# An attention and mixture-of-experts layer on one core: TensorE's scores products and values products stand between single items of the maximum pass, the latter in two parts

## The chip, the cores and the metric

The kernel runs on one core of one Trainium2 chip. The metric is the device time of one execution in microseconds (us); smaller is better.

## The reference

One layer on x of shape (4, 1024, 128), float32, with 16 heads of width 8, and then a mixture of 8 experts of which each token takes 2. Cut to what matters:

```python
Q, K, V = (proj(W_Q), proj(W_K), proj(W_V))          # (4, 16, 1024, 8)
Q = _apply_rope(Q, cos, sin)
K = _apply_rope(K, cos, sin)
scores = jnp.einsum('bhsd,bhtd->bhst', Q, K) / jnp.sqrt(jnp.float32(D_K))
scores = jnp.where(causal[None, None], scores, -jnp.inf)
attn = jax.nn.softmax(scores, axis=-1)
out = jnp.einsum('bhst,bhtd->bhsd', attn, V)
...
x = _layernorm(x + _L0_attn_ref(x, W_Q, W_K, W_V, W_O), axis=-1)
x = _layernorm(x + _L0_ffn_ref(x, Wg, bg, W1, b1, W2, b2), axis=-1)   # 8 experts, hidden 512, top 2
```

## The kernel before, in words

The attention works in 16 units, each of one batch and four heads. A unit is gone over twice. The **maximum pass** (events A, lines L703 to L708 on TensorE, L1157 on VectorE) computes the scores with the queries on the partitions and takes each query's maximum over the keys. It has 40 items per unit. An item is one head (or two, where the widths are small) of one block of 128 queries against up to 512 keys; its products fill one bank of a ring of three PSUM banks, and VectorE reduces that bank in one instruction. Where a block touches the diagonal, two small products (L703, L705) lay the mask under it first. The **second pass** computes the scores again, transposed, with the keys on the partitions and the maximum already subtracted (event QK, L734, two for each step, one for each pair of heads), takes the exponential on ScalarE (L867), cuts the diagonal block on GpSimd (L1408) and multiplies by the values (event PV, L754).

The second pass of a unit is 12 steps: for the first 512 queries four blocks of keys with 512, 384, 256 and 128 queries left of the diagonal, for the second 512 queries four with 512 and then four with 512, 384, 256 and 128. While the second pass of unit u runs, the maximum pass of unit u+1 is spread over its steps by a_quota, 1 to 5 items to a step (40 in all, as [4, 7, 10, 11, 15, 20, 24, 28, 33, 36, 38, 40] adds them up).

All engines walk the same written list of events (schedule()), each taking its own. So the order on every engine is fixed by that list, and an instruction that waits holds up all that stands behind it on its engine. In one step the list has: QK of the next step for the first pair of heads, half of the step's items, QK for the second pair, the other half, and then PV of the step before. PV is four products, one for each head, that stand side by side in the array's four groups of 32 columns (tile_position (0, 32 h)), float32, so that the trace shows eight instructions; QK and the items use the two halves of 64 rows, bfloat16: parity 0 of the heads lies on rows 0 to 63 and parity 1 on rows 64 to 127, so that two of different parity can run side by side.

What the waits in TensorE's list are: an item waits until VectorE has read the bank that it goes to (ring_read); QK i waits for the exponential of QK i-2 (exp_done); PV waits for both exponentials of its step, or for the two cuts on GpSimd where the step touches the diagonal (masked), and the first PV of each half of the queries waits in addition until ScalarE has copied the previous sum out of the one accumulator bank (ot_ready, event EV, L875). Beside these there are two small transposes a unit of the maxima (MT, L716, which wait for four small operations on GpSimd, L1379 to L1385, event SPLIT) and two of the results (OT, L763). From unit 4 on, the rest of the layer for the batch before (projection, norm, gating, scatter of the tokens by indirect DMA, L1394) is spread over the steps as well, and VectorE and TensorE have more to do; the steps from the last of unit 3 to the last but one of unit 11 are a loop body that runs twice. Unit 15 has no items beside it. After the attention come 72 tiles of the experts, which the change leaves alone.

Of the kernel before, what the change touches and what calls it, by code (L numbers as in the profile page):

```python
# [33 lines left out]
NG = H // GH  # L34
CH = 512
NCH = B * S // CH
# [54 lines left out]
B_STEPS = pass_b_steps()  # L91
NA, NB = len(A_ITEMS), len(B_STEPS)
NU = B * NG
C_LAST = [max(k for k, st in enumerate(B_STEPS) if st[0] == c) for c in range(2)]
# [5 lines left out]
def diagonal(k):  # L100

    c, j, s0, n = B_STEPS[k]
    return s0 == P * j


DIAG = [sum(diagonal(i) for i in range(k + 1)) for k in range(NB)]
# [5 lines left out]
    return [NA * sum(work[:i + 1]) // sum(work) for i in range(len(work))]  # L112


def schedule():

    quota = a_quota()
    ev = []
    ev.append(("VX", 0))
    first = next(k for k in range(NB) if quota[k] >= A_HALF)
    ev += [("A", 0, i) for i in range(A_HALF)] + [("SPLIT", 0, 0)]
    middle = (A_HALF + NA) // 2
    ev += [("A", 0, i) for i in range(A_HALF, middle)] + [("MT", 0, 0), ("MROWS", 0, 0)]
    ev += [("A", 0, i) for i in range(middle, NA)] + [("SPLIT", 0, 1)]  # L130
    ev += [("QK", 0), ("QK", 1)]

    def after(bt):

        order = [
            [("T1", bt, 0)], [("T1", bt, 1)], [("WO", bt, 0)], [("WO", bt, 1)],
            [("LNM", bt, 0)], [("LNM", bt, 1)], [("LNV", bt, 0)], [("LNR", bt, 0)], [("LNR", bt, 1)],
            [("LNA", bt, 0)], [("LNA", bt, 1)], [("T2", bt, 0)], [("T2", bt, 1), ("XC", bt), ("LG", bt, 0)], [("LG", bt, 1)],
            [("RA", bt, 0)], [("RX", bt), ("RS", bt, 0)], [("RB", bt, 0)], [("RB", bt, 1)],
            [("RC", bt, 0)], [("RC", bt, 1)], [("RK", bt, 0), ("RK", bt, 1)], [("RD", bt, 0)], [("RD", bt, 1)],  # L140
            [("RE", bt, 0)], [("RE", bt, 1)], [("RF", bt, 0)], [("RF", bt, 1)],
        ] + [[("SC", bt, i)] for i in range(2 * BT)] + ([[("SW", bt)]] if bt < B - 1 else [])
        plan = {3 + i: events for i, events in enumerate(order)}
        return plan

    for u in range(NU):
        for k in range(NB):
            step = u * NB + k
            items = []
            if u + 1 < NU:  # L150
                items = [("A", u + 1, n) for n in range(quota[k - 1] if k else 0, quota[k])]
            half = len(items) // 2
            if k == NB - 1 and u % NG == 3:
                ev.append(("MARK", u))
            if step + 1 < NU * NB:
                ev.append(("QK", 2 * step + 2))
            ev += items[:half]
            if step + 1 < NU * NB:
                ev.append(("QK", 2 * step + 3))
            ev += items[half:]  # L160
            if u + 1 < NU and k in (first, NB - 1):
                ev.append(("SPLIT", u + 1, int(k == NB - 1)))
            if step:
                ev.append(("PV", step - 1))
                if (step - 1) % NB in C_LAST:
                    ev.append(("EV", 2 * ((step - 1) // NB) + C_LAST.index((step - 1) % NB)))
            for back in (0, 1):

                if step >= 3 and (step - 3) % NB == C_LAST[back]:
                    ev.append(("OT", 2 * ((step - 3) // NB) + back))  # L170
            if k == 2 and u + 2 < NU:
                ev.append(("LOAD", u + 2))
            if k == 5 and u + 1 < NU:
                ev.append(("VX", u + 1))
            if k == first + 1 and u + 1 < NU:
                ev += [("MT", u + 1, 0), ("MROWS", u + 1, 0)]
            if k == 0:
                ev += [("MT", u, 1), ("MROWS", u, 1)]
            if u >= NG:
                ev += after(u // NG - 1).get(u % NG * NB + k, [])  # L180
            if u == NU - 1 and k == 4:
                ev.append(("TA",))
    last = NU * NB - 1
    ev += [("PV", last), ("EV", 2 * NU - 1), ("OT", 2 * NU - 1)]
    ev.append(("END",))
    for i, (_, events) in enumerate(sorted(after(B - 1).items())):
        ev += [("TILE", i)] + events

    r, out = 0, []
    for e in ev:  # L190
        if e[0] in ("A", "MT", "OT", "T1", "WO", "T2", "LG", "RK"):
            out.append((e, r))
            r += 1
        else:
            out.append((e, None))
    return out, r
# [75 lines left out]
def build(nc, xT, x, w, wg, bg, w1, w2,  # L272
          cs, ident, halves, maskA, before, tile128, tokens, tiles, first_row, out):
    ctx = ExitStack()
    with ctx:
# [140 lines left out]
        v_read = sem("v_read")  # L416
# [232 lines left out]
        def _(pe):  # L649
# [34 lines left out]
            def visit(e, r, at):  # L684
# [52 lines left out]
                elif kind == "PV":  # L737
                    u, k = divmod(e[1], NB)
                    c, j, s0, n = B_STEPS[k]
                    if e[1] == 0:  # L740
                        pe.wait_ge(v_read, NCH)
                    if k == 0:
                        pe.wait_ge(vx_ready, at(u + 1, NG))
                    if j == 0 and 2 * u + c > 0:

                        pe.wait_ge(ot_ready, at(2 * u + c, 2 * NG))
                    if diagonal(k):
                        pe.wait_ge(masked, at(2 * (u * DIAG[-1] + DIAG[k]), 2 * NG * DIAG[-1]))
                    else:
                        pe.wait_ge(exp_done, at(2 * e[1] + 2, 2 * NB * NG))  # L750
                    for slot_ in (0, 1):
                        for par in (0, 1):
                            h = 2 * slot_ + par
                            last = mm(pv[32 * h:32 * h + 32, s0 - c * CH:s0 - c * CH + n],  # L754
                                      vx[:, u % NG, j, h, :], probs[(2 * e[1] + slot_) % 6][:, par, 0:n],
                                      start=(j == 0), stop=(k == C_LAST[c]),
                                      tile_position=(0, 32 * h), skip_group_check=True)
                    last.then_inc(pv_done, 1)
                elif kind == "OT":
                    n = e[1]  # L760
                    pe.wait_ge(ot_ready, at(n + 1, 2 * NG))
                    for t in range(4):
                        last = nc.tensor.transpose(ring[:, bank, t * P:(t + 1) * P],  # L763
                                                   ot[:, n % 2, t * P:(t + 1) * P], id_sb[:, :])
                    last.then_inc(ring_full, 1)
                elif kind == "LG":
                    bt, c = e[1:]
                    pe.wait_ge(ring_read, at(RING_OF[("T2", bt, c)] + 1, RING_BATCH))
                    for t in range(4):
                        last = mm(ring[:, bank, t * E:(t + 1) * E], aT[:, c, t * P:(t + 1) * P], wg_sb[:, :],  # L770
                                  start=(t == 0), stop=True, skip_group_check=True)
                    last.then_inc(ring_full, 1)
                elif kind == "RK":

                    pe.wait_ge(top_mask, at(e[1] + 1, 1))
                    mm(ring[:, bank, 0:BT * E], before_sb[:, e[2], :], rt[:, 4, :, :], start=True, stop=True
                       ).then_inc(ring_full, 1)
                elif kind in ("T1", "WO", "T2"):
                    bt, c = e[1:]
                    if kind == "T1":  # L780

                        pe.wait_ge(ring_read, at(RING_OF[("OT", 2 * NG * bt + 2 * NG - 1)] + 1, RING_BATCH))
                    elif kind == "WO":
                        pe.wait_ge(ring_read, at(RING_OF[("T1", bt, c)] + 1, RING_BATCH))
                    else:
                        pe.wait_ge(x1_done, at(2 * bt + c + 1, 2))
                    for t in range(4):
                        cols = slice(t * P, (t + 1) * P)
                        if kind == "T1":
                            last = nc.tensor.transpose(ring[:, bank, cols], attn[:, 4 * c + t, :], id_sb[:, :])  # L790
                        elif kind == "WO":
                            last = mm(ring[:, bank, cols], aT[:, c, cols], w_sb[:, 5, :], start=(t == 0), stop=True,
                                      skip_group_check=True)
                        else:
                            last = nc.tensor.transpose(ring[:, bank, cols], xr[:, 4 * c + t, 0, 0:D], id_sb[:, :])
                    last.then_inc(ring_full, 1)
# [717 lines left out]
```

## Time and profile before

| | |
|---|---|
| median of 3 runs | 820.85 us (820.37 to 832.62) |
| the profiled execution | 823.58 us, span in the trace 821.8 us |
| TensorE (PE) busy | 683.3 us, 83% |
| VectorE (DVE) busy | 584.6 us, 71% |
| ScalarE (ACT) busy | 443.5 us, 54% |
| GpSimd (POOL) busy | 320.7 us, 39% |
| granted clock of TensorE | 0.90 on average |
| the attention's 16 units | about 74 to 592 us of the span |

"Busy" counts the time in which at least one instruction of the engine was under way. Products on TensorE are pipelined, and each row of it lasts longer than the distance to the next one's start; distances between starts tell what one costs when others follow.

### The profile page before, as it was taken

What the parts mean: (1) busy time and instruction counts of PE and PEld (TensorE: products, weight loads), DVE (VectorE), ACT (ScalarE), POOL (GpSimd) and SP (SyncE); (2) the same over time, 40 slices, a digit from 0 to 9 for tenths busy, and PEclk for the clock granted to TensorE, in tenths of its full rate; (3) what the DMA queues carried; (4) which work ended last, traced back from release to release, by engine and by line L of the source; (5) the groups of instructions that cost most, each with busy time, mean ns of one, the idle gap of its engine ahead of it and who ended that gap; (6) DMA issues with size and microseconds to landing.
All of it is one profiled execution on the core that took longest, in us unless ns stands there. A gap on an engine that the chain in (4) does not pass through costs nothing.

```text
span 821.8 us, 18980 instructions
## 1 busy us (share of the span) xinstructions
PE 683.3 (83%) x5560; PEld 362.6 (44%) x5561; DVE 584.6 (71%) x1467; ACT 443.5 (54%) x840; POOL 320.7 (39%) x577
## 2 busy tenths in 40 slices
PE   7987999999898868989889998988789857899830
PEld 3432333334343222434323333332278857798830
DVE  7886888888979867798988888896436712222266
ACT  2532676666455554556557655556647524466524
POOL 5961223322213265221328512226614555344551
PEclk9975999999879988998989998899989968899985
DMA  8893255011010120101012011000186745687923
GB/s 274 267 343 125 72 132 162 8 46 48 1 48 6 49 74 22 48 1 48 7 47 80 25 38 46 1 3 22 34 211 200 209 122 147 174 225 210 300 85 114
DMA packets 67352, 83.70 MB, mean 102 GB/s; under 512 B 9266, under 2 KB 46776, under 8 KB 67264
## 3 DMA queue, kind: packets, MB, share of 16 engines
q1 hardware_dynamic: 62912, 74.04, 30.5%
q0 software_dynamic: 4352, 8.53, 3.0%
q8 instruction: 49, 0.80, 0.4%
q14 instruction: 39, 0.32, 0.1%
HBM read 55.77 MB, written 26.90 MB: 101 GB/s over the span
## 4 chain that ended last, share of the span: by engine, by line
PE 50%; DVE 22%; issue 9%; ACT 5%; DMA 4%; SPq 4%; another core or an unknown queue 3%; POOL 2%; DVEq 0%; ACTq 0%; POOLq 0%
PE banks L754 14%; DVE mx L1157 14%; PE banks L708 9%; PE banks L823 6%; PE banks L734 5%; PE banks L812 5%; PE banks L703 2%; PE banks L763 2%; ACT region L867 2%; PE banks L655 2%; DMA region<-pairs 1%; ACT x_sb L910 1%; PE banks L832 1%; SPq L597 1%
## 5 line engine op out<-in xcount | busy, mean ns | idle before, releaser
L1157 DVE TENSOR_REDUCE mx<-banks 128x1 f32<-128x512 f32 (+3 forms) x640 | 366.0, 630 | 46.9 <-PE banks L708 41.5
L867 ACT ACTIVATE region<-banks 128x1024 f32<-128x1024 f32 (+3 forms) x256 | 201.3, 840 | 169.4 <-PE banks L734 159.7
L708 PE MATMUL banks<-region 64*128 64x512 bf16 (+3 forms) x768 | 196.0, 352 | 17.2 <-DVE mx L1157 15.1
L734 PE MATMUL banks<-region 64*128 64x512 bf16 (+3 forms) x768 | 141.6, 347 | 20.7 <-ACT region L867 11.4
L754 PE MATMUL banks<-region 128*32 128x512 f32 (+3 forms) x1024 | 123.1, 555 | 0.9 <-POOL region L1408 0.8
L867 ACT ACTIVATE cs_sb<-banks 128x1024 f32<-128x1024 f32 (+2 forms) x128 | 91.2, 759 | 42.4 <-PE banks L734 41.8
L1418 POOL DMA_INDIRECT results<-region,dest x72 | 71.7, 996 | 105.1 <-DVE region L1285 71.9
L703 PE MATMUL banks<-mask_sb,half_sb 64*128 64x128 bf16 (+1 forms) x384 | 84.7, 252 | 22.6 <-DVE mx L1157 17.3
L1279 DVE TENSOR_TENSOR region<-banks,w1e 128x128 f32<-128x128 f32 x72 | 21.0, 291 | 110.8 <-PE banks L812 66.3
L823 PE MATMUL banks<-region,w1e 128*128 128x128 f32 x576 | 83.2, 291 | 19.3 <-ACT region L893 13.9
L1408 POOL TENSOR_SCALAR_AFFINE_SELECT region<-region 128x256 f32<-128x256 f32 x160 | 64.2, 410 | 87.7 <-ACT region L867 85.1
L734 PEld LDWEIGHTS banks<-region 64*128 64x128 bf16 x768 | 42.4, 95 | 122.9 <-issue 47.3
L1408 POOL TENSOR_SCALAR_AFFINE_SELECT cs_sb<-cs_sb 128x256 f32<-128x256 f32 x96 | 38.6, 412 | 143.4 <-ACT cs_sb L867 142.6
L708 PEld LDWEIGHTS banks<-region 64*128 64x128 bf16 x768 | 65.2, 100 | 56.0 <-DVE mx L1157 42.9
L812 PE MATMUL banks<-w_sb,region 128*128 x576 | 83.3, 290 | 3.9 <-issue 1.8
L823 PEld LDWEIGHTS banks<-region,w1e 128*128 128x128 f32 x576 | 75.9, 205 | 21.4 <-ACT region L893 15.6
L901 ACT ACTIVATE region<-banks,w1e 128x128 f32<-128x128 f32 x288 | 82.9, 379 | 0.5 <-PE banks L823 0.5
L812 PEld LDWEIGHTS banks<-w_sb,region 128*128 128x128 f32 x576 | 74.3, 200 | 8.1 <-issue 6.7
L1394 POOL DMA_INDIRECT pairs<-xT_sb,slot x64 | 63.0, 985 | 36.9 <-issue 21.8
L705 PE MATMUL banks<-mask_sb,half_sb 64*128 64x64 bf16 (+1 forms) x384 | 71.3, 209 | 0.0
L893 ACT COPY region<-banks 128x128 f32<-128x128 f32 x72 | 19.2, 267 | 93.1 <-PE banks L832 67.5
L703 PEld LDWEIGHTS banks<-mask_sb,half_sb 64*128 64x128 bf16 x384 | 35.2, 97 | 61.9 <-DVE mx L1157 46.4
(177 smaller groups left out, 687.8 us busy)
## 6 DMA issues: line engine op xcount, KB each, us to landing
w1e<-in_w SPq DMA_DIRECT2D x72, 322.0 KB
region<-stack_q SPq DMA_DIRECT2D x64, 112.0 KB
region<-stack_k SPq DMA_DIRECT2D x32, 224.0 KB
region<-pairs SPq DMA_DIRECT2D x72, 66.0 KB
region<-results SPq DMA_DIRECT2D x8, 512.0 KB, 4.9
stack_q<-x_sb SPq DMA_DIRECT2D x8, 384.0 KB, 3.6
stack_k<-x_sb SPq DMA_DIRECT2D x8, 384.0 KB, 4.5
stack_q<-x_sb SPq DMA_DIRECT2D x8, 256.0 KB, 3.9
```

What stands on the lines that cost most here:

```text
L703: mm(view[:, :, n - P:n], half_sb[rows, 0, :], mask_sb[rows, 0, 0:k, :], start=True, stop=False, skip_group_check=True)
L705: mm(view[:, :, n - P // 2:n], half_sb[rows, 1, :], mask_sb[rows, 1, 0:k, P // 2:P], start=False, stop=False, skip_group_check=True)
L708: last = mm(ring[:, bank, m * n:(m + 1) * n], qst[rows, v % NG, sb_ // 4, slot_, sb_ % 4 * P:(sb_ % 4 + 1) * P], kst[rows, v % NG, slot_, ...
L734: last = mm(score[:, slot_, par, 0:n], kst[rows, u % NG, slot_, j * P:(j + 1) * P], qst[rows, u % NG, c, slot_, s0 - c * CH:s0 - c * CH + ...
L754: last = mm(pv[32 * h:32 * h + 32, s0 - c * CH:s0 - c * CH + n], vx[:, u % NG, j, h, :], probs[(2 * e[1] + slot_) % 6][:, par, 0:n], start ...
L812: last = mm(down[k % 2], hg[:, k % 2, hc * P:(hc + 1) * P], w2_sb[:, bass.ds(e, 1), hc, :].rearrange("p a n -> p (a n)"), start=(hc == 0), ...
L823: last = mm(hidden[k % 2][:, hc * P:(hc + 1) * P], w1e[:, k, hc * P:(hc + 1) * P], xgT[:, k % 2, :], start=(hc == 0), stop=(hc == HC - 1), ...
L867: nc.scalar.activation(probs[i % 6][:, :, 0:n], score[:, i % 2, :, 0:n], ACT.Exp, scale=SCALE).then_inc(exp_done, 1)
L901: nc.scalar.activation(hg[:, k % 2, cols], hidden[k % 2][:, cols], ACT.Gelu_apprx_tanh, bias=w1e[:, k, HID + hc:HID + hc + 1]).then_inc(ge ...
L1157: read(v.tensor_reduce(dst, src, AX.X, ALU.max, negate=True))
L1408: pp.affine_select(out=block_, in_=block_, compare_op=ALU.is_ge, fill=0.0, base=0, pattern=[[0, 2], [1, P]], channel_multiplier=-1).then_i ...
L1418: pp.indirect_dma_start(out=results, out_offset=bass.IndirectOffsetOnAxis(ap=dest[:, k, :], axis=0), in_=ys[:, k, :], in_offset=None, boun ...
```

## The change

In each step the list now mixes scores products, values products and items singly. PV of a step with more than 256 queries is cut into two parts of half the queries each (eight of the twelve steps); the others stay whole. The sequence is QK, PV part 0, QK, PV part 1, with a quarter of the step's items (two, one or none) behind each of the four; where the PV is whole there are three places. Where PV belongs to the first step of a half of the queries (it waits for the accumulator), both QK come first. The waits of PV stand at its first part, its count for others at its last.

```diff
+def pv_parts(step):
+    return (0, 1) if B_STEPS[step % NB][3] > CH // 2 else (1,)
...
-            half = len(items) // 2
...
-            if step + 1 < NU * NB:
-                ev.append(("QK", 2 * step + 2))
-            ev += items[:half]
-            if step + 1 < NU * NB:
-                ev.append(("QK", 2 * step + 3))
-            ev += items[half:]
+            scores = [("QK", 2 * step + 2 + i) for i in (0, 1)] if step + 1 < NU * NB else []
+            values = [("PV", step - 1, i) for i in pv_parts(step - 1)] if step else []
+            if step and B_STEPS[(step - 1) % NB][1] == 0:
+                mixed = scores + values
+            else:
+                mixed = [e for i in (0, 1) for e in scores[i:i + 1] + values[i:i + 1]]
+            for i, e in enumerate(mixed):
+                ev.append(e)
+                ev += items[len(items) * i // len(mixed):len(items) * (i + 1) // len(mixed)]
             if u + 1 < NU and k in (first, NB - 1):
                 ev.append(("SPLIT", u + 1, int(k == NB - 1)))
-            if step:
-                ev.append(("PV", step - 1))
-                if (step - 1) % NB in C_LAST:
-                    ev.append(("EV", 2 * ((step - 1) // NB) + C_LAST.index((step - 1) % NB)))
+            if step and (step - 1) % NB in C_LAST:
+                ev.append(("EV", 2 * ((step - 1) // NB) + C_LAST.index((step - 1) % NB)))
...
+                    n0, n1 = (0, n) if len(parts_) == 1 else (n // 2 * e[2], n // 2 * (e[2] + 1))
                     for slot_ in (0, 1):
                         for par in (0, 1):
                             h = 2 * slot_ + par
-                            last = mm(pv[32 * h:32 * h + 32, s0 - c * CH:s0 - c * CH + n],
-                                      vx[:, u % NG, j, h, :], probs[(2 * e[1] + slot_) % 6][:, par, 0:n],
-                                      start=(j == 0), stop=(k == C_LAST[c]),
+                            last = mm(pv[32 * h:32 * h + 32, s0 - c * CH + n0:s0 - c * CH + n1],
+                                      vx[:, u % NG, j, h, :], probs[(2 * e[1] + slot_) % 6][:, par, n0:n1],
+                                      start=(j == 0 and n0 == 0), stop=(k == C_LAST[c] and n1 == n),
                                       tile_position=(0, 32 * h), skip_group_check=True)
-                    last.then_inc(pv_done, 1)
+                    if e[2] == parts_[-1]:
+                        last.then_inc(pv_done, 1)
```

The order moves on TensorE alone; on the other engines the rows are the same. In the changed kernel the lines of TensorE are six or ten further down: the items are L709, L711 and L714, QK is L740, PV is L764.

TensorE in the middle of a unit, a step of 512 queries (in the trace of before this is the step from 149.13 us). L734 is QK, L708 an item or two, L754 PV (four heads). Before:

```order
L734 MATMUL banks<-region 128x512 x2
L708 MATMUL banks<-region 128x512 x2
L734 MATMUL banks<-region 128x512 x2
L708 MATMUL banks<-region 128x512 x2
L754 MATMUL banks<-region 32x512 x4
```

The same step now (L740 is QK, L714 an item, L764 half a PV):

```order
L740 MATMUL banks<-region 128x512 x2
L714 MATMUL banks<-region 128x512
L764 MATMUL banks<-region 32x256 x4
L714 MATMUL banks<-region 128x512
L740 MATMUL banks<-region 128x512 x2
L714 MATMUL banks<-region 128x512
L764 MATMUL banks<-region 32x256 x4
L714 MATMUL banks<-region 128x512
```

The items no longer stand in pairs, and the four heads' products come twice with half the queries.

TensorE two steps later, with short QK (the step from 154.84 us). Before:

```order
L734 MATMUL banks<-region 128x256 x2
L708 MATMUL banks<-region 128x512
L734 MATMUL banks<-region 128x256 x2
L708 MATMUL banks<-region 128x512 x2
L754 MATMUL banks<-cs_sb,region 32x512 x4
```

Now:

```order
L740 MATMUL banks<-region 128x256 x2
L764 MATMUL banks<-cs_sb,region 32x256 x4
L714 MATMUL banks<-region 128x512
L740 MATMUL banks<-region 128x256 x2
L714 MATMUL banks<-region 128x512
L764 MATMUL banks<-cs_sb,region 32x256 x4
L714 MATMUL banks<-region 128x512
```

The first half of PV has moved to directly behind the first QK, ahead of all three items.

## Rows read from the trace of the kernel before

**Rows 1.** The page: busy time by engine, and the granted clock in 40 slices (tenths).

```profile
PE 683.3 (83%) x5560; PEld 362.6 (44%) x5561; DVE 584.6 (71%) x1467; ACT 443.5 (54%) x840; POOL 320.7 (39%) x577
...
PEclk9975999999879988998989998899989968899985
```

**Rows 2.** Busy time by stretch (PE, PEld, DVE, ACT, POOL), granted clock, DMA.

```profile
140.71:168.44 27.73, 25.66 (x250) 9.67 (x250) 24.34 (x48) 18.90 (x27) 8.41 (x25) 1.00 0.11 35
207.00:241.00 34.00, 29.82 (x255) 13.13 (x253) 30.51 (x81) 19.08 (x26) 8.59 (x25) 0.86 0.09 29
...
480.00:520.00 40.00, 36.05 (x288) 15.82 (x286) 33.77 (x87) 21.43 (x28) 8.49 (x25) 0.85 0.08 25
520.00:555.00 35.00, 30.71 (x261) 11.23 (x259) 31.27 (x86) 19.46 (x27) 8.61 (x25) 0.94 0.01 2
```

**Rows 3.** TensorE's instructions in order of time, 140 to 168 us: each step's first QK, some others.

```profile
142.12 0.39 PE L734 MATMUL banks<-region 64*128 64x512 bf16 x2
...
144.48 1.07 PE L754 MATMUL banks<-region 128*32 128x512 f32 x8
145.48 0.26 PE L716 MATMUL banks<-idb_sb,msp 128*96 128x128 bf16 x1
145.67 0.39 PE L734 MATMUL banks<-region 64*128 64x512 bf16 x2
...
149.13 0.39 PE L734 MATMUL banks<-region 64*128 64x512 bf16 x2
149.35 0.38 PE L708 MATMUL banks<-region 64*128 64x512 bf16 x2
...
151.83 0.34 PE L734 MATMUL banks<-region 64*128 64x384 bf16 x2
...
154.84 0.39 PE L734 MATMUL banks<-region 64*128 64x256 bf16 x3
...
156.59 0.23 PE L734 MATMUL banks<-region 64*128 64x128 bf16 x2
...
157.91 0.39 PE L734 MATMUL banks<-region 64*128 64x512 bf16 x2
...
159.42 0.34 PE L734 MATMUL banks<-region 64*128 64x384 bf16 x2
...
162.24 0.28 PE L734 MATMUL banks<-region 64*128 64x256 bf16 x2
...
164.05 0.28 PE L734 MATMUL banks<-region 64*128 64x128 bf16 x3
...
166.19 0.61 PE L734 MATMUL banks<-region 64*128 64x512 bf16 x4
...
166.72 0.38 PE L708 MATMUL banks<-region 64*128 64x512 bf16 x1
167.02 0.64 PE L754 MATMUL banks<-cs_sb,region 128*32 128x256 f32 x8
167.70 0.39 PE L734 MATMUL banks<-region 64*128 64x512 bf16 x2
```

**Rows 4.** VectorE's instructions in order of time, same unit; idle time ahead in brackets.

```profile
140.69 4.94 DVE L1157 TENSOR_REDUCE mx<-banks 128x1 f32<-128x512 f32 x9 [0.61 <-PE banks L708]
...
152.45 2.55 DVE L1157 TENSOR_REDUCE mx<-banks 128x1 f32<-128x384 f32 x5 [0.20 <-PE banks L708]
155.38 3.08 DVE L1157 TENSOR_REDUCE mx<-banks 128x1 f32<-128x512 f32 x5 [0.38 <-PE banks L708]
```

**Rows 5.** Who waited for whom in the unit 140.71 to 168.44: total us, times, longest.

```profile
DVE mx L1157 <- PE banks L708: 3.3, 10, 0.6
...
PE banks L716 <- POOL msp L1385: 0.6, 1, 0.6
```

**Rows 6.** VectorE's waits from 81 to 592 us: total us, times, longest.

```profile
DVE mx L1157 <- PE banks L708: 33.9, 81, 2.8
DVE rden L1170 <- PE banks L763: 12.4, 17, 4.2
```

More of the change, by code:

```diff
@@ L183, in schedule @@
     last = NU * NB - 1
-    ev += [("PV", last), ("EV", 2 * NU - 1), ("OT", 2 * NU - 1)]
+    ev += [("PV", last, i) for i in pv_parts(last)] + [("EV", 2 * NU - 1), ("OT", 2 * NU - 1)]
     ev.append(("END",))
@@ L739, in visit @@
                     c, j, s0, n = B_STEPS[k]
[L740 to L750, printed above, removed]
+                    parts_ = pv_parts(e[1])
+                    if e[2] == parts_[0]:
+                        if e[1] == 0:
+                            pe.wait_ge(v_read, NCH)
+                        if k == 0:
+                            pe.wait_ge(vx_ready, at(u + 1, NG))
+                        if j == 0 and 2 * u + c > 0:
+                            pe.wait_ge(ot_ready, at(2 * u + c, 2 * NG))
+                        if diagonal(k):
+                            pe.wait_ge(masked, at(2 * (u * DIAG[-1] + DIAG[k]), 2 * NG * DIAG[-1]))
+                        else:
+                            pe.wait_ge(exp_done, at(2 * e[1] + 2, 2 * NB * NG))
+                    n0, n1 = (0, n) if len(parts_) == 1 else (n // 2 * e[2], n // 2 * (e[2] + 1))
                     for slot_ in (0, 1):
```

## The prediction

> **What bounds the kernel now.** I read the page first [rows 1], then the stretches [rows 2], then one unit of the attention instruction by instruction. The page names no single engine: TensorE 83% busy, VectorE 71%, and TensorE's busy time is not time at its peak. The experts' part is outside the change; what matters is 74 to 592 us. There the two are close together. In the unit from 140.71 to 168.44 us VectorE is busy 24.34 of 27.73 us and TensorE 25.66 [rows 2]. In the later units, with the rest of the layer beside them, VectorE is busy 30.5 of 34 and 31.3 of 35 us [rows 2], so VectorE leads there.
>
> How they hinder each other is seen in the starts of QK, which mark TensorE's steps [rows 3]. From 142.12 us on the twelve steps take 3.55, 3.46, 2.70, 3.01, 1.75, 1.32, 1.51, 2.82, 1.81, 2.14, 1.51 us; the twelfth, from 167.70 us, brings the sum to the period of 27.73 us, so 2.15. Six long steps make 17.7 us, six short ones 10.0. An item costs VectorE 0.60 us: five in 3.08 us [rows 4], less the 0.08 by which the last one's record is longer than that distance. In the long steps 4 or 5 items want 2.4 to 3.0 us, and TensorE is stopped by full banks. Then PV comes in one piece, the three banks run dry, and VectorE waits 0.2 to 0.6 us for the first item behind it [rows 4]; ten such waits make 3.3 us of the unit [rows 5]. In the short steps (2 or 3 items) TensorE has no pause at all: its own work sets their length.
>
> **The edits.** All of them are on TensorE; each is priced by distances between starts.
>
> Cutting PV. A bunch of PV with 512 queries holds the array 1.00 us, 144.48 to 145.48 [rows 3]. Its record lasts 1.07 us and that with 256 queries 0.64, so 256 queries less are 0.43 less: a half holds it 0.57 us. (167.02 to 167.70 gives 0.68 for 256 queries, with a wait possibly in it.) Ahead of a bunch there is a price too. Items or QK follow each other at 0.22 us (149.13 to 149.35), but PV starts 0.30 us behind the last item (166.72 to 167.02): 0.08. One bunch costs 1.08, two halves 1.30: 0.22 us for each cut. Eight cuts a unit and 16 units are 128 cuts, 28 us of TensorE's time. The bounds, were there no such overhead or were the 0.68 right: 0 and 56 us. I take 28, since two rows of whole bunches give it.
>
> What the rows show here is a price of some 0.1 us at each change between the 64-row products and PV. The Trainium skill (TensorEngine Tiling (Array Packing), Key Properties) says that changing the tiling mode drains the array. If the drain cost the whole tail by which a record outlasts the distance to the next (0.39 less 0.22, 0.17 us), the changes counted below would cost 3.6 us a unit where the rows make it 2.3; by the rows the forecast stands, by the rule it would be some 20 us higher.
>
> Single items. Two items of different parity run side by side in 0.22 us, the record x2 at 149.35 [rows 3]. By the written order a unit has 11 such pairs now and 2 afterwards. A single item is not all loss: one of parity 1 lies beside the first product of the QK behind it, and the second product beside the next item. Counted through, with 0.22 us for 512 columns and 0.11 for each change of mode (28 in a unit before, 49 after), TensorE's own work grows by 21 x 0.11 = 2.3 us for the changes and, of 9 x 0.22 = 2.0 us of lost pairs, by about 1.3: together **3.6 us a unit**, from about 23.1 to 26.7 us.
>
> Where that lies on the path. In the short steps all of it: four of the six have a cut PV, and each gets 0.22 for the cut and 0.22 for a lost pair, 1.8 us together. In the long steps TensorE waits for banks anyway. There a half step (an item beside half of QK, QK beside an item, half a PV: 0.22 + 0.22 + 0.08 + 0.57 = 1.1 us) supplies two items in less than the 1.2 us that VectorE takes for them, so with three banks VectorE should not run dry. I give back 1.5 us: half of the 3.3 us [rows 5], the waits in the long steps. I do not take all, for the length of two long steps is set elsewhere: 159.42 to 162.24 contains 0.6 us for the maxima's split on GpSimd [rows 5], and the one from 167.70 the copy of the accumulator. Net +0.3 us for a unit like this one.
>
> Moved waits. PV now stands in front of items that do not need it. It wants exponentials that the QK ahead of it has nearly waited for already; the cut on GpSimd comes after the exponential. Price 0 where ScalarE is ahead, 0.2 us where not; cover: the QK ahead. If GpSimd is behind with the scatters (units 7, 11, 15), items behind PV stop too. I take 0, up to 0.3 us twice a unit (10 us) for the range. VectorE, ScalarE, GpSimd and the DMA queues keep their orders, so nothing there is moved past anything.
>
> **The sum.** Units 0 to 3, 7 and 11 are of the kind counted: 6 x 0.3 = 2 us. Units 4, 8, 12 (projection beside) the same: 1 us. Six units are led by VectorE; at full clock the additions hide in TensorE's waits, 0. But the clock is down to 0.85 and 0.86 there [rows 2]: at the lower level for 9.5 of 34 us and 12 of 40, about 60 us over all such units by the digits of [rows 1]. TensorE at half speed leads, and its own work is up by 3.6 in 27.7 us, 13%; I take half of 8 us, 4. Unit 15 has no items to put between, only cuts: 1 us. Together +8 us, on the profiled execution's 823.6 us; that one lies 2.7 us above the median, and 820.85 + 7 or 8 gives **828 us**, 1% slower, which this kernel's measurement can hardly tell from no change (2%, 16 us, is about what it can tell).
>
> **Rivals.** (1) Finer steps feed VectorE: faster. VectorE's waits for items and for the results' transposes are 33.9 and 12.4 us [rows 6]. If three banks bridge every half PV, a good half goes, 26 us, and the added TensorE work lies in its waits: 796 us. For it: VectorE leads in most later units, and the half step of 1.1 us is below 1.2. Against it: the short steps, in which TensorE has nothing to hide behind. Chance 0.16.
>
> (2) TensorE becomes the bound: slower. Its own 26.7 us a unit leave 1 us of a period of 27.7. Waits of the kind that stay (GpSimd's split, the copy, single full banks) were 27.7 - 23.1 = 4.6 us a unit; if 2.6 of them stay instead of about 1.3, a unit takes 29.3, 1.6 us more, and 15 units 24 us: 845 us. It decides when more than about 1.1 us a unit is added. For it: every item now stands behind the one before, no burst can catch up. Chance 0.27.
>
> (3) The clock. Where the array stays occupied, the clock stayed at its upper level: 1.00 in the early unit [rows 2]. Denser work might keep it up later. The Trainium skill (TensorE: Matmul & The Clock Gate, HAM oscillation) warns of small pauses between groups of products, which are what the change spreads or removes. All 60 us at the lower level gone would be about 12 us by the 20% by which such stretches seem slowed (34 us against 27.7, mostly other work): 816 us. Chance 0.07.
>
> (4) The order has no effect, since full banks hold TensorE until the same moments: 821 us. Chance 0.05. The forecast itself has 0.45.
>
> **Range and chances.** From 804 us (part of rival 1) to 848 us (rival 2 with its waits); beyond lie most of rival 1 and the upper end of the cut's price. Faster by over 2% (below 804): 0.15. Within 2%: 0.57. Slower by over 2% (above 837): 0.28.
>
> **What would show it.** In the profile after: halves of PV (256 queries) with 0.57 us to the next start; the unit's period 28.0 us where it was 27.73; VectorE's ten waits of 3.3 us a unit down to about 1.8; the short steps 0.4 us longer, the long ones shorter; TensorE's waits for VectorE shorter. I would be wrong if halves hold the array 0.45 or 0.7 us, if the short steps do not grow, or if VectorE's waits do not shrink at all.

## The result and the profile after

The changed kernel takes 839.83 us (median of 4 runs, 838.2 to 841.77) against 823.13 us before (4 runs): ratio 1.018, 95% interval 1.014 to 1.022. Slower, by 16.7 us between the medians; whether by more than 2% this interval leaves open. The profiled execution has a span of 836.6 us against 821.8.

The page after: busy time, granted clock, and the group of the items on VectorE (busy and mean ns, then idle time ahead and what ended it).

```profile
PE 713.3 (85%) x6584; PEld 381.5 (46%) x6585; DVE 585.9 (70%) x1467; ACT 452.4 (54%) x840; POOL 321.5 (38%) x577
...
PEclk9966999999979989697879998899979977999985
...
L1168 DVE TENSOR_REDUCE mx<-banks 128x1 f32<-128x512 f32 (+3 forms) x640 | 372.9, 630 | 82.2 <-PE banks L714 72.1
```

TensorE is busy 30 us longer than in [rows 1]; VectorE's busy time is nearly the same (585.9 and 584.6), but it waits longer. Stretches of the changed kernel, columns as in [rows 2]:

```profile
130.90:159.60 28.70, 27.62 (x320) 11.23 (x317) 24.55 (x48) 19.55 (x26) 8.46 (x25) 1.00 0.18 53
...
261.60:294.10 32.50, 29.59 (x322) 11.78 (x320) 30.24 (x80) 19.70 (x26) 12.03 (x28) 1.00 0.13 38
409.50:446.90 37.40, 34.74 (x322) 13.52 (x318) 30.84 (x80) 19.95 (x27) 11.82 (x28) 0.82 0.10 32
```

The steady unit has grown from 27.73 us [rows 2, 3] to 28.70, TensorE's busy time in it by 2 us. TensorE of the changed kernel in order of time, each step's first QK (L740) and some others, as in [rows 3]:

```profile
130.87 0.39 PE L740 MATMUL banks<-region 64*128 64x512 bf16 x1
...
132.66 0.34 PE L740 MATMUL banks<-region 64*128 64x384 bf16 x2
...
135.76 0.39 PE L740 MATMUL banks<-region 64*128 64x256 bf16 x4
...
137.83 0.23 PE L740 MATMUL banks<-region 64*128 64x128 bf16 x1
...
140.61 0.39 PE L740 MATMUL banks<-region 64*128 64x512 bf16 x2
...
142.12 0.39 PE L740 MATMUL banks<-region 64*128 64x512 bf16 x2
...
143.95 0.39 PE L740 MATMUL banks<-region 64*128 64x512 bf16 x2
...
147.49 0.39 PE L740 MATMUL banks<-region 64*128 64x512 bf16 x2
...
151.39 0.39 PE L740 MATMUL banks<-region 64*128 64x512 bf16 x2
151.61 0.38 PE L714 MATMUL banks<-region 64*128 64x512 bf16 x1
151.92 0.64 PE L764 MATMUL banks<-region 128*32 128x256 f32 x8
152.49 0.39 PE L714 MATMUL banks<-region 64*128 64x512 bf16 x1
152.49 0.60 PE L740 MATMUL banks<-region 64*128 64x512 bf16 x2
152.72 0.38 PE L714 MATMUL banks<-region 64*128 64x512 bf16 x1
153.03 0.64 PE L764 MATMUL banks<-region 128*32 128x256 f32 x8
153.60 0.33 PE L740 MATMUL banks<-region 64*128 64x384 bf16 x1
...
156.01 0.29 PE L740 MATMUL banks<-region 64*128 64x256 bf16 x2
...
157.81 0.44 PE L740 MATMUL banks<-region 64*128 64x128 bf16 x2
...
159.58 0.39 PE L740 MATMUL banks<-region 64*128 64x512 bf16 x1
```

A half PV holds the array 0.57 us (151.92 to 152.49; 153.03 to 153.60) and starts 0.31 us behind the last item (151.61 to 151.92; 152.72 to 153.03). The lengths of the steps are the differences of the starts of QK. In the table they are set beside those of [rows 3], beginning with the step whose QK is a unit's first. The list writes QK one step ahead, so that column 1 belongs to the last step of the list and column n, from 2 on, to the list's step n-1. Short steps in the sense of the prediction are columns 1, 3, 4, 5, 11 and 12, long ones 2 and 6 to 10. (The sum of rounded starts is 28.71 where the period below is 28.70.)

| step | 1 | 2 | 3 | 4 | 5 | 6 | 7 | 8 | 9 | 10 | 11 | 12 | sum |
|---|---|---|---|---|---|---|---|---|---|---|---|---|---|
| before | 1.51 | 2.82 | 1.81 | 2.14 | 1.51 | 2.15 | 3.55 | 3.46 | 2.70 | 3.01 | 1.75 | 1.32 | 27.73 |
| after | 1.79 | 3.10 | 2.07 | 2.78 | 1.51 | 1.83 | 3.54 | 3.90 | 2.21 | 2.41 | 1.80 | 1.77 | 28.71 |

VectorE in the same unit of the changed kernel, idle time in brackets:

```profile
136.43 0.56 DVE L1168 TENSOR_REDUCE mx<-banks 128x1 f32<-128x384 f32 x1 [0.35 <-PE banks L714]
137.35 0.56 DVE L1168 TENSOR_REDUCE mx<-banks 128x1 f32<-128x384 f32 x1 [0.36 <-PE banks L714]
```

And its waits in the unit 130.9 to 159.6 (total us, times, longest):

```profile
DVE mx L1168 <- PE banks L714: 4.0, 11, 0.8
```

In columns 3 and 4 an item arrives about every 0.9 us (136.43 to 137.35), with half a PV between each two, where VectorE's record of one lasts 0.56. So its waits are 4.0 us where they were 3.3 [rows 5], and from 82 to 607 us

```profile
DVE mx L1168 <- PE banks L714: 63.2, 127, 3.0
```

where [rows 6] had 33.9. Interleaving was to make VectorE wait less; it waits more. Run 8 below shows why: TensorE has become the slower of the two.

### The profile page after: what moved, and what is told of

Same layout as the page of the kernel before. It is cut to its first block, busy times and chain, and to the rows that moved or that the text cites. A ratio compares the mean times of both kernels' runs of the same rounds, so it can differ in the third digit from the quotient of the medians.

```text
span 836.6 us, 21028 instructions
## 1 busy us (share of the span) xinstructions
PE 713.3 (85%) x6584; PEld 381.5 (46%) x6585; DVE 585.9 (70%) x1467; ACT 452.4 (54%) x840; POOL 321.5 (38%) x577
## 4 chain that ended last, share of the span: by engine, by line
PE 54%; DVE 18%; issue 8%; ACT 5%; SPq 5%; DMA 3%; another core or an unknown queue 3%; POOL 2%; DVEq 0%; ACTq 0%; POOLq 0%
PE banks L764 15%; DVE mx L1168 11%; PE banks L714 10%; PE banks L740 6%; PE banks L823 5%; PE banks L834 5%; PE banks L709 4%; PE banks L774 2%; ACT region L878 2%; ACT cs_sb L878 1%; SPq L603 1%; DMA region<-pairs 1%; ACT x_sb L921 1%; SPq L597 1%
## 5 line engine op out<-in xcount | busy, mean ns | idle before, releaser
L1168 DVE TENSOR_REDUCE mx<-banks 128x1 f32<-128x512 f32 (+3 forms) x640 | 372.9, 630 | 82.2 <-PE banks L714 72.1
L878 ACT ACTIVATE region<-banks 128x1024 f32<-128x1024 f32 (+3 forms) x256 | 208.9, 840 | 178.3 <-PE banks L740 169.3
L714 PE MATMUL banks<-region 64*128 64x512 bf16 (+3 forms) x768 | 217.0, 352 | 9.3 <-DVE mx L1168 7.7
L740 PE MATMUL banks<-region 64*128 64x512 bf16 (+3 forms) x768 | 179.3, 346 | 11.2 <-DMA region<-mparts 4.2
L764 PE MATMUL banks<-region 128*32 128x256 f32 (+2 forms) x1792 | 141.8, 392 | 0.9 <-POOL region L1419 0.8
L878 ACT ACTIVATE cs_sb<-banks 128x1024 f32<-128x1024 f32 (+2 forms) x128 | 93.9, 759 | 52.2 <-PE banks L740 46.4
L709 PE MATMUL banks<-mask_sb,half_sb 64*128 64x128 bf16 (+1 forms) x384 | 93.9, 256 | 14.8 <-DVE mx L1168 11.2
L714 PEld LDWEIGHTS banks<-region 64*128 64x128 bf16 x768 | 67.1, 100 | 72.7 <-DVE mx L1168 44.1
L834 PEld LDWEIGHTS banks<-region,w1e 128*128 128x128 f32 x576 | 74.1, 201 | 23.5 <-ACT region L904 19.0
L709 PEld LDWEIGHTS banks<-mask_sb,half_sb 64*128 64x128 bf16 x384 | 35.1, 96 | 104.8 <-DVE mx L1168 64.9
L711 PE MATMUL banks<-mask_sb,half_sb 64*128 64x64 bf16 (+1 forms) x384 | 78.6, 212 | 0.0
L1405 POOL DMA_INDIRECT pairs<-xT_sb,slot x64 | 63.0, 985 | 32.5 <-issue 19.8
L740 PEld LDWEIGHTS banks<-region 64*128 64x128 bf16 x768 | 47.0, 95 | 46.5 <-issue 23.9
```

The source lines that it names most:

```text
L709: mm(view[:, :, n - P:n], half_sb[rows, 0, :], mask_sb[rows, 0, 0:k, :], start=True, stop=False, skip_group_check=True)
L711: mm(view[:, :, n - P // 2:n], half_sb[rows, 1, :], mask_sb[rows, 1, 0:k, P // 2:P], start=False, stop=False, skip_group_check=True)
L714: last = mm(ring[:, bank, m * n:(m + 1) * n], qst[rows, v % NG, sb_ // 4, slot_, sb_ % 4 * P:(sb_ % 4 + 1) * P], kst[rows, v % NG, slot_, ...
L740: last = mm(score[:, slot_, par, 0:n], kst[rows, u % NG, slot_, j * P:(j + 1) * P], qst[rows, u % NG, c, slot_, s0 - c * CH:s0 - c * CH + ...
L764: last = mm(pv[32 * h:32 * h + 32, s0 - c * CH + n0:s0 - c * CH + n1], vx[:, u % NG, j, h, :], probs[(2 * e[1] + slot_) % 6][:, par, n0:n1 ...
L834: last = mm(hidden[k % 2][:, hc * P:(hc + 1) * P], w1e[:, k, hc * P:(hc + 1) * P], xgT[:, k % 2, :], start=(hc == 0), stop=(hc == HC - 1), ...
```

## The experiments

Edits are shown against the changed kernel; that of runs 7 to 11 is the same line in each. Ratios are to the kernel before, of 10 executions each in runs 1 to 4 and 12 in run 6; the other runs have one execution each. Units 1 to 3 have the same length to 0.01 us in each kernel here, so the steady period can be told to about that. It is the distance of two rows of the transpose of the maxima, one unit apart. Before, in TensorE's order of time:

```profile
134.35 0.23 PE L716 MATMUL banks<-idb_sb,msp 128*96 128x128 bf16 x1 [0.62 <-POOL msp L1385]
...
162.08 0.23 PE L716 MATMUL banks<-idb_sb,msp 128*96 128x128 bf16 x1 [0.62 <-POOL msp L1385]
```

Changed kernel (28.70 us):

```profile
135.60 0.23 PE L722 MATMUL banks<-idb_sb,msp 128*96 128x128 bf16 x1 [0.59 <-POOL msp L1396]
...
164.30 0.23 PE L722 MATMUL banks<-idb_sb,msp 128*96 128x128 bf16 x1 [0.60 <-POOL msp L1396]
```

"Changes" and "pairs" below are counts of one unit in the order of the program: changes between 64-row products, PV and transposes, and items of parity 0 directly followed by parity 1. The prediction and the expectations say 49 changes for the changed kernel and 33, 45 and 32 for runs 2, 5 and 6; the lists, and TensorE's rows in the traces, have 48, 32, 44 and 31. It alters none of the expectations by more than 0.11 us.

**1. Cut, but one part behind the other.** PV in two parts at its old place:

```diff
-            for i, e in enumerate(mixed):
-                ev.append(e)
-                ev += items[len(items) * i // len(mixed):len(items) * (i + 1) // len(mixed)]
+            half = len(items) // 2
+            ev += scores[0:1] + items[:half] + scores[1:2] + items[half:]
...
+            ev += values
```

> The order of before, PV cut in two parts that stand one behind the other. The changes between kinds of products stay 28 in a unit, the pairs of items 11. Theory A (a cut costs only through the two changes between the 64-row products and PV, which are not there here): period of a steady unit 27.73 to 27.9 us, time within 0.4% of before (about 824 us). Theory B (the cut costs 0.22 us by itself, through four more loads and starts): four short steps longer by 0.22 us each, period 28.6 us, 836 us.

Measured: ratio 0.999 (0.996 to 1.002), period 27.76 us:

```profile
135.36 0.23 PE L722 MATMUL banks<-idb_sb,msp 128*96 128x128 bf16 x1 [0.61 <-POOL msp L1396]
...
163.12 0.23 PE L722 MATMUL banks<-idb_sb,msp 128*96 128x128 bf16 x1 [0.62 <-POOL msp L1396]
```

The cut costs nothing by itself, the four more weight loads and products of each included. Theory B falls.

**2. Whole PV between single items.**

```diff
-    return (0, 1) if B_STEPS[step % NB][3] > CH // 2 else (1,)
+    return (1,)
```

> PV whole, but standing between single items: 33 changes a unit, 5 pairs. Theory A (short steps pay for changes and lost pairs alike, long steps gain by finer supply): +5 changes x 0.11 and 6 lost pairs, of which half counts, against a smaller gain than with halves: period 27.8 to 28.2 us, 824 to 830 us. Theory C (the lost pairs are what costs, 9 of them made the 1.7 us of the short steps): 6 of 9, period 28.2 to 28.6, 830 to 836 us. If changes alone cost: 27.5 us, 820 us.

Measured: ratio 0.996 (0.992 to 0.999), period 27.46 us:

```profile
135.63 0.23 PE L722 MATMUL banks<-idb_sb,msp 128*96 128x128 bf16 x1 [0.59 <-POOL msp L1396]
...
163.09 0.23 PE L722 MATMUL banks<-idb_sb,msp 128*96 128x128 bf16 x1 [0.60 <-POOL msp L1396]
```

Moving PV and taking the items apart is a small gain of 0.4%, just clear of noise, and the period is the shortest of all with full reductions. My theory A (27.8 to 28.2) missed, and so did C (28.2 to 28.6): six of the nine lost pairs are lost here too, so that pairs alone are not the cause. What came out is what I had written for the case that changes alone cost, 27.5 us. The loss of the changed kernel lies in what this run leaves out: the cuts that stand apart, and with them 16 changes and the last three pairs.

**3. Cut, with the items in their halves.** The order is QK, half the items, part 0, QK, half the items, part 1:

```diff
-            for i, e in enumerate(mixed):
-                ev.append(e)
-                ev += items[len(items) * i // len(mixed):len(items) * (i + 1) // len(mixed)]
+            half = len(items) // 2
+            late = step and B_STEPS[(step - 1) % NB][1] == 0
+            ev += scores[0:1] + items[:half] + ([] if late else values[0:1])
+            ev += scores[1:2] + items[half:] + (values if late else values[1:])
```

> PV in two parts, one behind each half of the step's items, the items of a half together as before: 41 changes, 11 pairs. Theory A: the cuts cost 4 x 0.22 = 0.9 us in the short steps, the long ones keep some 0.7 us of gain, period 27.9 us, about 826 us. Theory C (pairs alone cost): the gain stands without the loss, period 27.0 us, 813 us. If the changes cost more than the rows say: 28.5 us, 835 us.

Measured: ratio 0.997 (0.993 to 1.000), period 27.90 us, as theory A had it:

```profile
135.66 0.23 PE L723 MATMUL banks<-idb_sb,msp 128*96 128x128 bf16 x1 [0.68 <-POOL msp L1397]
...
163.56 0.23 PE L723 MATMUL banks<-idb_sb,msp 128*96 128x128 bf16 x1 [0.68 <-POOL msp L1397]
```

With 13 changes more than before it costs 0.17 us a unit, and the whole kernel (821 us where I expected 826) is not slower at all. In its profiled execution TensorE was at the lower clock for 52 us of units 0 to 14 where it was for 69 in that of before, which may hide the 0.17; no run separates the two.

**4. The new order in three long steps alone.**

```diff
+def mixes(k):
+    return k in (4, 7, 8)
...
+            if not mixes(k):
+                half = len(items) // 2
+                mixed = []
+                ev += scores[0:1] + items[:half] + scores[1:2] + items[half:]
```

In the steps that do not mix, PV stands whole at its old place.

> The new order in three of the twelve steps alone (the fifth, eighth and ninth of a unit, those that became 0.32, 0.48 and 0.60 us shorter in the steady unit), the old one in the other nine: 32 changes, 7 pairs. Theory A (each step gains or loses for itself): period 26.3 us, and 15 units give 21 us less than before: 802 us. Rival D (the gain of a long step was borrowed: its neighbour starts with emptier banks and gives it back): period 27.4 to 27.7 us, 818 to 823 us.

Measured: ratio 0.999 (0.995 to 1.002), period 27.71 us. My theory A missed by 20 us; rival D came out. TensorE of this kernel (QK is L751):

```profile
151.08 0.39 PE L751 MATMUL banks<-region 64*128 64x512 bf16 x2
...
153.30 0.33 PE L751 MATMUL banks<-region 64*128 64x384 bf16 x1
...
155.71 0.29 PE L751 MATMUL banks<-region 64*128 64x256 bf16 x2
...
158.46 0.23 PE L751 MATMUL banks<-region 64*128 64x128 bf16 x2
```

The three steps are columns 6, 9 and 10 of the table. Columns 9 and 10 take 2.22 and 2.41 us as in the changed kernel, and the short one behind them 2.75 instead of 1.75. TensorE had run ahead of VectorE and waits for it there: from 155.6 to 158.6 us the weight loads of its items (L725) wait three times for VectorE, 1.3 us together.

**5. The complement: the new order in the nine other steps**, k not in (4, 7, 8).

> The complement of the fourth: the new order in the nine other steps, the old one in the fifth, eighth and ninth; 45 changes, 6 pairs. If each step gains or loses for itself: steady period 28.7 + 1.4 = 30.1 us. If long steps only borrow from their neighbours, as the fourth showed (27.71): 28.6 to 28.9 us.

Measured: one execution, 840.81 us; period 29.78 us.

```profile
140.25 0.23 PE L733 MATMUL banks<-idb_sb,msp 128*96 128x128 bf16 x1 [0.59 <-POOL msp L1407]
...
170.03 0.23 PE L733 MATMUL banks<-idb_sb,msp 128*96 128x128 bf16 x1 [0.60 <-POOL msp L1407]
```

I expected 28.6 to 28.9 from run 4, and missed. The same three steps are worth nothing beside the old order (27.73 to 27.71) and 1.08 us beside the new one (29.78 to 28.70). In the old order VectorE takes back what TensorE saves; beside the new one TensorE is the limit, and what columns 9 and 10 save counts. The whole kernel does not show it: 840.8 us is what the changed kernel takes too, though 15 units should make 16 us. By the traces' clock records TensorE was at the lower level for 47 us of units 0 to 14 here and for 80 in the changed kernel; one execution does not tell how much of the 16 us that is.

**6. Whole PV in the middle, items in halves.** Run 3 with PV whole.

> The corner that is missing beside the changed kernel (28.70), the second (27.46) and the third (27.90): PV whole, in the middle of the step, the items in their halves as before; 32 changes, 11 pairs. If cuts and lost pairs add up: cut 1.24 by the single-item row, pairs 0.80 by the cut row, so 26.7 to 27.0 us a unit and about 812 us. If a whole PV between items already leaves VectorE as the limit: 27.2 to 27.5 us, 819 us. If the moved PV brings a wait of its own: above 27.73, over 823 us.

Measured: ratio 1.005 (1.003 to 1.008), period 27.81 us:

```profile
135.10 0.23 PE L723 MATMUL banks<-idb_sb,msp 128*96 128x128 bf16 x1 [0.67 <-POOL msp L1397]
...
162.91 0.23 PE L723 MATMUL banks<-idb_sb,msp 128*96 128x128 bf16 x1 [0.67 <-POOL msp L1397]
```

The two effects do not add up (26.7 to 27.0 was wrong). Here no step is cut, and it is slower than run 2 with its five pairs. The period lies where I had put a wait of the moved PV itself, but the trace has no such wait: TensorE's waits in this unit are for VectorE and, 0.7 us, for the split.

**7 to 11. TensorE's own time.** To see it, VectorE's reduction is made short in five orders: it reads the first 64 columns of each head of an item, so that the maxima are those of fewer keys.

```diff
-                    read(v.tensor_reduce(dst, src, AX.X, ALU.max, negate=True))
+                    read(v.tensor_reduce(dst, src[:, :, 0:64], AX.X, ALU.max, negate=True))
```

What remains is not TensorE's work alone: its waits for GpSimd and ScalarE stay in it, 1.4 us in run 7 and 1.3 in run 8. "Own time" below means the period with them.

In the order of before:

> The order of before, but VectorE reduces only the first 64 columns of each head of an item, so that the maxima are those of fewer keys. It takes VectorE's limit away and leaves TensorE's own time, with what GpSimd and ScalarE put in. Predicted own time 23.1 us a unit; with the 0.6 us for the split about 24 us. If TensorE was not near its limit: under 22 us.

```profile
129.81 0.23 PE L716 MATMUL banks<-idb_sb,msp 128*96 128x128 bf16 x1 [0.65 <-POOL msp L1385]
...
154.97 0.23 PE L716 MATMUL banks<-idb_sb,msp 128*96 128x128 bf16 x1 [0.65 <-POOL msp L1385]
```

In that of the changed kernel:

> The same shortened reduction in the changed kernel. By the count of changes and pairs its own time is 26.7 us a unit, 3.6 more than the one before: about 27.3 us. If the added work of TensorE is smaller and the loss comes from waits for VectorE: under 25.5 us.

```profile
137.42 0.23 PE L722 MATMUL banks<-idb_sb,msp 128*96 128x128 bf16 x1 [1.00 <-POOL msp L1396]
...
165.67 0.23 PE L722 MATMUL banks<-idb_sb,msp 128*96 128x128 bf16 x1 [1.00 <-POOL msp L1396]
```

25.16 and 28.25 us (whole kernels 741.5 and 780.8 us, one execution each), where I expected about 24 and 27.3: both are some 1 us longer, the difference of 3.1 is near the 3.3. VectorE's full reductions add 2.57 us to the first and 0.45 to the second. This is the answer to where the time went: the change adds **3.1 us** to TensorE's own unit. Of these 2.1 go into time in which it waited for VectorE before, and 1.0 makes the period longer. Step by step, in the columns of the table above (TensorE's starts of QK, one unit of each trace):

| step | 1 | 2 | 3 | 4 | 5 | 6 | 7 | 8 | 9 | 10 | 11 | 12 |
|---|---|---|---|---|---|---|---|---|---|---|---|---|
| before, short (7) | 1.51 | 2.81 | 1.81 | 2.13 | 1.51 | 1.83 | 2.91 | 2.99 | 2.24 | 2.35 | 1.75 | 1.32 |
| changed, short (8) | 1.79 | 3.09 | 2.07 | 2.78 | 1.51 | 1.83 | 3.54 | 3.45 | 2.22 | 2.41 | 1.80 | 1.76 |

Against the table above this shows who sets each step. Before, the short reduction shortens columns 6 to 10 and no other: there TensorE waited for VectorE. In the changed kernel eleven columns keep their length to 0.01 us, and the whole 0.45 us is in column 8 (3.90 to 3.45).

In the orders of runs 3, 2 and 6:

> VectorE reduces the first 64 columns only, in the order of the third (cut, items in halves: 41 changes, 11 pairs). TensorE's own steady period was 25.17 us in the order of before (28 changes, 11 pairs) and 28.25 in the changed one (49, 2). With 0.11 us for a change and the rest for pairs: 25.17 + 13 x 0.11 = 26.6 us. If changes cost half of that and the pairs the rest: 25.9 us.

```profile
131.15 0.23 PE L723 MATMUL banks<-idb_sb,msp 128*96 128x128 bf16 x1 [1.01 <-POOL msp L1397]
...
157.65 0.23 PE L723 MATMUL banks<-idb_sb,msp 128*96 128x128 bf16 x1 [1.01 <-POOL msp L1397]
```

> The same shortened reduction in the order of the second (PV whole, single items: 33 changes, 5 pairs). With 0.11 us for a change and 0.085 for a pair: 25.17 + 0.55 + 0.51 = 26.2 us. With half the price for a change and 0.2 for a pair: 26.7 us.

```profile
138.84 0.26 PE L722 MATMUL banks<-idb_sb,msp 128*96 128x128 bf16 x1
...
164.10 0.26 PE L722 MATMUL banks<-idb_sb,msp 128*96 128x128 bf16 x1
```

> The same shortened reduction in the order of the sixth (PV whole, in the middle, items in halves: 32 changes, 11 pairs): 25.17 + 4 x 0.11 = 25.6 us; with half the price 25.4 us. The sixth kernel, with whole reductions, took 27.81 us, so that VectorE and not TensorE would set its period.

Its period is 25.40 us, by two such rows at 139.97 and 165.37 us. Runs 9 and 11 came out at 26.50 and 25.40 where I expected 26.6 and, at half the price, 25.4; run 10 took 25.26 where I expected 26.2 or 26.7, and missed. All orders side by side, in us of a steady unit:

| order | changes | pairs | short reductions | whole reductions | VectorE adds |
|---|---|---|---|---|---|
| before | 28 | 11 | 25.16 | 27.73 | 2.57 |
| whole PV between, singles (2, 10) | 32 | 5 | 25.26 | 27.46 | 2.20 |
| whole PV between, halves (6, 11) | 31 | 11 | 25.40 | 27.81 | 2.41 |
| cut, halves (3, 9) | 41 | 11 | 26.50 | 27.90 | 1.40 |
| changed: cut, singles (8) | 48 | 2 | 28.25 | 28.70 | 0.45 |

Two things follow. A price per change and one per pair do not describe the middle column: six pairs fewer cost nothing where PV is whole (25.40 to 25.26), but the cut costs 1.10 us with halves (0.14 for each of 8 cuts on average) and 2.99 with singles (0.37 for each, with the three lost pairs). Over the steps it is uneven: with halves column 12 alone grows from 1.30 to 1.85 us, half of the 1.10, and columns 7 and 11 grow by nothing. And the right-hand columns show how the two engines are coupled: up to 26.5 us of TensorE's own time the period hardly moves (27.46 to 27.90), since most of what TensorE adds goes into its waits for VectorE; at 28.25 it lies only 0.45 above TensorE. Between 26.5 and 28.25 no order was run.

## Why the prediction was right, and where it was off

The direction (slower) and the range held: 828 us forecast, 840 measured, in a range of 804 to 848. But the loss is 16.7 us where I had 7 or 8, and what happened is nearer to my rival 2, TensorE becomes the bound (845 us), than to the forecast's own balance. That the measured time lies within the range is owed in part to its width.

**What bounds the kernel now.** Right for the short steps, in which TensorE and not VectorE sets the length: run 7 leaves them as they are, and all but column 5 grew. Right that TensorE waits for VectorE in the long ones, except column 2, which I had put down to the split on GpSimd and which run 7 leaves alone too. Column 6, which I had put down to the copy of the accumulator, gets 0.32 us shorter.

**Cutting PV.** The halves hold the array 0.57 us, and PV starts 0.31 us behind an item, to 0.01 us as forecast. That the price is not in the cut itself is shown by run 1: adjacent halves cost 0.03 us a unit. The Trainium skill (TensorEngine Tiling (Array Packing), Key Properties) says that a change of tiling mode, not of tile alone, drains the array; the runs agree in kind, with nothing for the cut without a change (run 1) and 1.10 us for the cuts with ten changes more (run 9 against 11). In size the rows decide: on average 0.14 us a cut where items stand in halves and 0.37 where they stand singly, on either side of the 0.22 I took.

**Single items.** TensorE's own unit was to grow by 3.6 us and grew by 3.1 (with 20 changes more, not 21). The division into 2.3 for changes and 1.3 for pairs was wrong, for the two are no separate items. In the rows of the changed kernel a lone item ahead of PV takes 0.31 us for one product (151.61 to 151.92), while one beside QK starts together with a product of it (152.49), and four products fit into the 0.54 us up to 153.03. That a lone item costs only next to a change is how I read this and the 0.14 and 0.37; no run varies it alone.

**Where that lies on the path: the step that failed.** "I give back 1.5 us" was mis-sized. The short steps paid 0.28, 0.26, 0.64, 0.00, 0.05 and 0.45 us, together 1.68, where 1.8 was forecast. The long steps gave back 0.32, 0.01, 0.49 and 0.60, and two of them grew instead, by 0.28 and 0.44: net 0.70. I had let the long steps only shrink, as if VectorE were their limit in both orders. With 3 us more of its own work TensorE is the limit in them as well: in the changed kernel only column 8 gets shorter with the short reduction. Its own time in columns 2, 7 and 8 grew by 0.28, 0.63 and 0.46 us (runs 7 and 8), so that little or nothing was left to give back there; in 6, 9 and 10 it did not grow by more than 0.06. Net +0.98 us a unit where I had +0.3.

Fifteen times 0.98 would be 14.7 us, and from the first QK of unit 0 to that of unit 15 the profiled executions take 494.05 us before (73.63 to 567.68) and 508.48 after (74.27 to 582.75), 14.4 more. But that the two agree is partly chance. Units 1 to 3 grow by 0.97 or 0.98 each; the others change by between -1.9 and +5.3 us, and the clock, below, has a share in that.

**VectorE's waits** were to fall to 1.8 us a unit. They rose to 4.0, which I had named as a sign that I would be wrong. TensorE's visible waits for VectorE did fall as forecast, from 0.7 to 0.3 us.

**Moved waits.** 0 was right: in the unit TensorE's waits for GpSimd are the same 0.6 us. **Unit 15** was put at 1 us: from its first QK to that of its last step it takes 22.30 us before and 23.28 after, 0.98 more.

**The clock.** Between 74 and 592 us before, and 74 and 607 after, these stretches show it:

```profile
74.00:328.00 254.00, 225.65 (x2026) 87.31 (x2022) 212.06 (x455) 153.69 (x210) 82.93 (x212) 0.93 0.19 54
328.00:592.00 264.00, 232.61 (x2017) 91.99 (x2021) 218.70 (x534) 157.55 (x214) 96.94 (x224) 0.93 0.10 31
```

```profile
74.00:330.00 256.00, 237.54 (x2538) 97.45 (x2538) 212.69 (x455) 158.77 (x210) 83.26 (x212) 0.95 0.19 54
330.00:607.00 277.00, 253.62 (x2521) 104.31 (x2525) 219.67 (x534) 161.27 (x214) 96.26 (x222) 0.90 0.09 30
```

At the lower level (1.2 GHz, half) were, by these rounded figures, 36 + 37 = 73 us before and 26 + 55 = 81 after; the clock records of the two traces add up to 72 and 84. What it costs is seen in two units of the changed kernel with the same work: 32.5 us at clock 1.00 and 37.4 at 0.82, the last two stretches in the section on the result; 2 x 0.18 x 37.4 = 13.5 us at the lower level for 4.9 us. So the 12 us more are worth some 4 us, an estimate from this one pair of units. The denser order did not keep the clock up (rival 3). Its gain in the steady unit was none, since that was at 1.00 before. The units led by VectorE, in which I put 0 at full clock, are mixed by this. Of two of them the one at clock 1.00 takes 32.5 us against 33.9 before at clock 0.95, the later one, at 0.82, 37.4 against 34.3 at 0.90. Which unit meets a low clock was not controlled.

## What to carry to other kernels

Before work is spread out to feed a waiting engine, count what the spreading adds to the feeder and compare it with the feeder's own time, not with its waits: here 3.1 us were added where 2.6 were free, and only 2.1 of these could be used. Shortening the other engine's work in an experiment shows that own time, with its waits for the remaining engines, step by step, and tells whether a saved or added microsecond will count. A gain seen in one step is no gain until the period shows it: the same three steps were worth 0.02 us in one order and 1.08 in the other.

## What the runs showed of the hardware beyond that

Cutting a product of four column groups (float32, 512 queries) in two adjacent halves is free: 27.76 against 27.73 us a unit. With 64-row products between the halves a cut costs 0.14 us of TensorE's own time on average, and 0.37 where the items stand singly (table of runs 7 to 11).

With the short reductions the granted clock stayed up far more, with the same program on TensorE. The stretch of the units in the order of before:

```profile
74.00:508.50 434.50, 404.29 (x4035) 170.37 (x4039) 211.74 (x989) 308.05 (x423) 176.78 (x434) 0.97 0.17 50
```

That is about 26 us at the lower level instead of 73 (22 instead of 72 by the clock records); in the changed kernel it is 16 instead of 84. So shortening VectorE's work took most of the low stretches away, in one execution of each. What TensorE did before each fall of the clock is not shown here. Its waits for VectorE alone do not tell: in the changed kernel they are 18 us from 81 to 592 us where they were 31, and it has 12 us more at the lower level.
